# A quantized last layer on one NeuronCore: ScalarE writes the normalized rows, and the block maxima are taken over absolute values in one pass

## The reference

```python
def _mx_quantize(t, eps=1e-30):
    blocks = t.reshape(rows, K // 32, 32)
    scales = jnp.maximum(jnp.max(jnp.abs(blocks), axis=-1) / 7.5, eps)
    q = _nearest_on_grid(blocks / scales[..., None], _GRID)   # the 6-bit grid E2M3
    return (q, scales)

x = x + L1_attn(layernorm(x))       # state-space layer: delta, decay, scan, output
x = x + L1_ffn(layernorm(x))        # xd = xq * xs, wd = wq * ws, xd @ wd.T + bias
```

## Time and profile before

| | us |
|---|---|
| three runs | 3044.51, 3052.33, 3056.43 (median 3052.33) |
| the profiled execution | 3045.67 |
| its span in the trace | 3043.5 |
| PE busy | 2498.7 (82%) |
| DVE busy | 2124.9 (70%) |
| ACT busy | 1605.3 (53%) |
| POOL busy | 1112.7 (37%) |

### The profile page before, as it was taken

The page is one execution under the profiler, slowest core; times in us unless marked ns, Lnnn a source line. Parts: engine busy times, 40 slices in busy tenths (PEclk is TensorE's granted clock), DMA queues, the critical chain, the costliest instruction groups (busy, mean ns, idle before and its releaser), DMA issues. The chain is left out here.

```text
span 3043.5 us, 109358 instructions
## 1 busy us (share of the span) xinstructions
PE 2498.7 (82%) x45968; PEld 1887.2 (62%) x45968; DVE 2124.9 (70%) x5160; ACT 1605.3 (53%) x2896; POOL 1112.7 (37%) x1092
## 2 busy tenths in 40 slices
PE   4578887788888878788778999999978898987665
PEld 2345555556565555555566888888867676765443
DVE  4878988899889999888835222222325676878996
ACT  5454555555465554455124555555546666665442
POOL 0000233333333333233433777777744333332000
PEclk8778888888888898788679999999999899999877
DMA  2000122122222122113235999998798575754431
GB/s 66 8 11 10 49 74 71 53 79 75 71 74 73 55 79 73 63 69 111 84 114 172 301 310 305 306 305 296 258 336 305 202 275 209 268 217 173 161 107 28
DMA packets 191579, 448.61 MB, mean 147 GB/s; under 512 B 34034, under 2 KB 83700, under 8 KB 182772
## 3 DMA queue, kind: packets, MB, share of 16 engines
q1 hardware_dynamic: 129652, 284.26, 28.5%
q0 software_dynamic: 52224, 148.97, 12.9%
q10 hardware_dynamic: 9216, 8.39, 0.9%
HBM read 266.07 MB, written 175.42 MB: 145 GB/s over the span
## 5 line engine op out<-in xcount | busy, mean ns | idle before, releaser
L1041 POOL DMA_INDIRECT scr_xs<-xn_r,idx x512 | 534.1, 1043 | 1136.8 <-PE ps L473 479.7
L1068 POOL DMA_INDIRECT scr_ys<-y,idx_t x576 | 578.4, 1004 | 548.0 <-ACT sg L1333 253.1
L712 PE MATMUL ps<-xT,wr 128*128 128x256 f32 (+1 forms) x2560 | 563.5, 364 | 4.7 <-DVE h L2053 4.7
L2053 DVE TENSOR_TENSOR h<-sg,ps 128x256 f32<-128x256 f32 x320 | 125.2, 393 | 532.8 <-ACT sg L1333 532.2
L712 PEld LDWEIGHTS ps<-xT,wr 128*128 128x128 f32 x2560 | 439.1, 193 | 56.1 <-issue 14.1
L720 PE MATMUL ps<-wr,h 128*128 128x256 f32 x1152 | 312.3, 390 | 56.4 <-ACT y L1340 56.3
L1340 ACT ACTIVATE y<-ps,of_row 128x256 f32<-128x256 f32 x576 | 244.8, 471 | 145.2 <-PE ps L720 139.8
L720 PEld LDWEIGHTS ps<-wr,h 128*128 128x128 f32 x1152 | 218.5, 195 | 89.3 <-issue 62.1
L1680 DVE TENSOR_TENSOR tu<-tu,tmp 128x60 f32<-128x60 f32 (+14 forms) x480 | 242.5, 505 | 16.5
L527 PE MATMUL ps<-sq,w_proj 128*128 128x512 f32 x512 | 249.7, 624 | 5.1 <-issue 2.4
L1677 DVE TENSOR_TENSOR tmp<-tu 128x60 f32<-128x60 f32 (+14 forms) x480 | 241.6, 503 | 13.4
(11 more groups left out here) (268 smaller groups left out, 4231.6 us busy)
## 6 DMA issues: line engine op xcount, KB each, us to landing
wr<-in_wexp SPq DMA_DIRECT2D x224, 384.0 KB, 4.5
xt<-scr_xs SPq DMA_DIRECT2D x256, 280.0 KB, 4.2
yg<-scr_ys SPq DMA_DIRECT2D x64, 1024.0 KB, 7.4
scr_ys<-y,idx_t POOLq DMA_INDIRECT x576
scr_xs<-zeros SPq DMA_DIRECT2D x64, 140.0 KB
xt<-scr_xs SPq DMA_DIRECT2D x64, 140.0 KB
x_in<-in_x SPq DMA_DIRECT2D x64, 128.0 KB, 3.1
x_res<-in_x SPq DMA_DIRECT2D x64, 128.0 KB, 2.6
```

The costliest lines, as they stand in the source:

```text
L712: last = pe.matmul(ps[:, bank, half * TILE:half * TILE + wide], wr[:, w % NW, at:at + EI], xT2[:, t % NH, k, 0:wide], start=k == 0, stop=k ...
L1041: nc.gpsimd.indirect_dma_start(xs[int(i >= FIRST)][:, :], bass.IndirectOffsetOnAxis(idx[:, i % NR, c, k:k + 1], 0), xn_r[:, i % NR, c, :], ...
L1068: nc.gpsimd.indirect_dma_start(ys[int(t >= NTH[0])][:, :], bass.IndirectOffsetOnAxis(idx_t[:, t % NRT, r:r + 1], 0), y2[:, t % NY, r, :], ...
```

## The change

The four normalizing instructions of a round go from VectorE to ScalarE, which computes `x * std + off` with `off = -mean * std` in place of `(x - mean) * std`. VectorE therefore makes `off` for the quantized layer with a new small instruction (`quant_offsets`), between the tail statistics and `add("QO", i - 1)`. ScalarE's new `quant_rows(i)` stands behind the two roots and ahead of `share(2)` and `tail_rows(i + 1)`, and waits for `off` and for the turns of the `xq` before. VectorE waits for the rows on a new semaphore ahead of `quantize`. In `quantize`, the masking of the sign bit into `qb` and the maximum over `qb` become one reduction over `qa` with `apply_absolute_value`; this holds for the weight too.

```diff
+            def quant_rows(i):
+                if i:
+                    ring.filled(act, "QT1", i - 1)
+                act.wait_ge(s_off["quant"], i + 1)
+                for c in range(NC):
+                    last = nc.scalar.activation(xq[:, c, :], x3[:, i % NX3, c, :], ACT.Identity,
+                                                bias=off["quant"][:, c:c + 1], scale=std["quant"][:, c:c + 1])
+                last.then_inc(s_rows, 1)
...
                 root("quant", i)
                 if i + 1 < NB:
                     root("tail", i + 1)
+                quant_rows(i)
                 share(2)
                 if i + 1 < NB:
                     tail_rows(i + 1)
...
-            def normalize(dst, src, ph, i, st):
-                dve.wait_ge(s_std[ph], i + 1)
-                for c in range(NC):
-                    last = V.tensor_scalar(dst[:, c, :], src[:, c, :], mv[ph][:, c, 0:1],
-                                           std[ph][:, c:c + 1], ALU.subtract, ALU.mult)
-                    if c < NC - 1:
-                        st.did(last)
-                return last
...
-                st.did(V.tensor_scalar(qb.bitcast(I32), qa.bitcast(I32), 0x7FFFFFFF, None, ALU.bitwise_and))
-                st.wait(dve)
-                st.did(V.tensor_reduce(qs[:, 0:n, 0], blk(qb), AX.X, ALU.max))
+                st.did(V.tensor_reduce(qs[:, 0:n, 0], blk(qa), AX.X, ALU.max, apply_absolute_value=True))
                 st.wait(dve)
...
+            def quant_offsets(i):
+                offsets("quant", i)
+
             def quant_rows(i):
-                if i:
-                    ring.filled(dve, "QT1", i - 1)
-                sQ.did(normalize(xq, x3[:, i % NX3], "quant", i, sQ))
                 share(1)
-                sQ.wait(dve)
+                dve.wait_ge(s_rows, i + 1)
                 quantize(xq[:].rearrange("p c d -> p (c d)"), qb[:], qc[:], NC * D // QB, sQ, share)\
                     .then_inc(s_xn["quant"], 1)
...
                 share(1)
+                quant_offsets(i)
                 if i:
                     add("QO", i - 1)
```

More of the change, by code:

```diff
@@ L370, in network_kernel @@
         s_route = sem("s_route")
+        s_rows = sem("s_rows")
         s_x1 = sem("s_x1")
```

## The result

The kernel after takes 3059.68 us in the median of 20 runs against 3051.17 us for 20 runs of the kernel before beside it: ratio 1.0031, 95% interval 1.0021 to 1.0042, so 9.5 us more by the ratio (6 to 13; the medians are 8.5 apart). I had forecast 3077 us, +24.6, with a range of 3055 to 3097. The median lies inside the range, near its lower end, and the sign is right; the size is two and a half times too large. The ratio's interval lies above 1, so the loss is real, though smaller than the 15 us that I had said a measurement could tell from no change. The profiled execution took 3059.06 us, 13.4 more than that of before.

The account below looks back on a forecast made before the run. The bound was taken as a ring of waits through ScalarE, VectorE and TensorE; 10.4 + 2.4 + 6.8 + 7.1 - 2.1 = +24.6 us on the 3052.33 us median gave 3077 us, range 3055 to 3097.

Parts of the forecast that it names:

- the ring: Tail rounds: chain of engines waiting on each other, statistics to `xa` included; four added ScalarE activations, 2.07 to 2.08 us, delay it.
- Round 0 and the odd rounds: Rounds 0, 1, 3, 5, 7: ScalarE has no gap before `xa`, so 2.09 us each passes on in full, 10.4 us.
- The even rounds: Rounds 2, 4, 6, 8: ScalarE had 1.69 us to spare ahead of `xa`, so only 0.6 us each, 2.4 us.
- The clock in the mixed stage: Rounds 1 to 8: longer waits for `xa` lower TensorE's clock, 1.7 us in four of the eight, 6.8 us.
- The bare stage: Rounds 9 to 14, running alone: `xa` 1.47 us later each, 8.8 us less 1.8 of scan slack, +7.1 us; clock 0.
- VectorE's saving: About 2.0 us less VectorE work a round, 32 us over 16 rounds, worth 0 except in round 15.
- The end: Round 15: the removed normalizing and mask are on the path, 1.41 + 0.73 us, so -2.1 us.
- The one-pass maximum: In `quantize`: absolute-value reduction taken as 1.22 us, bounds 0.69 and 1.91; only round 15 would feel it, -0.5 to +0.7 us.
- (b): Rival for the whole tail: the order costs but TensorE's clock doesn't, +17.8 us, 3070 us; chance 0.22.
- The no-change form of (a): Rival: VectorE's saving gains in rounds 9 to 15 alone, cancelling the +12.8 us of earlier rounds, 3051 us; chance 0.10.
- VectorE as the bound everywhere: Rival: VectorE sets the time in all rounds, so its 32 us less work is gained, 3020 us; chance 0.05.
- The short form: Rival's part for rounds 9 to 15: VectorE's saving counts there, 6 x -2.0 - 2.1 = -14 us; no-change chance 0.10.

Follow-up runs that it names:

- `mixed_only`: Changed kernel with ScalarE writing the normalized rows in rounds 0 to 8 alone, VectorE normalizing in 9 to 15, sign mask kept: ratio 1.0034 to before.
- `late_mixed`: Rows on ScalarE in rounds 0 to 8 alone, mask kept, but placed behind the copies of the turned `xa`, ahead of softplus: ratio 0.9998 to before.
- `double`: Changed kernel with ScalarE writing the four rows once more each round into a tile that nobody reads: ratio 1.0163 to before.
- `before_again`: The kernel before, unchanged, traced a second time: 208.6 us from scan 9 to scan 15, against 208.5 in the first trace.
- `half_bare`: Rounds 0 to 8 as before; in 9 to 15 ScalarE writes the four rows plus two again into an unread tile: ratio 1.004 to before.
- `bare_only`: Changed kernel with ScalarE writing the rows in rounds 9 to 15 alone, rounds 0 to 8 and the mask as before: ratio 0.9993 to before.
- `abs_only`: The kernel before with only the one-pass reduction over absolute values in place of mask and maximum: ratio 1.0002 to before.
- `behind`: Changed kernel with ScalarE's rows directly behind the next block's `xa`, ahead of the copies of its turns, in all rounds: ratio 1.0057 to before.
- `best_dve`: Before with one-pass maximum; rounds 10 to 15 reordered (tail root and `xa` first, one table load dropped, `combine`s moved), VectorE normalizing throughout: 3031.98 us, ratio 0.9967.

## Why the prediction was right in sign and wrong in size

**ScalarE's rows sit on the ring: right.** The four activations took 2.06 us (forecast 2.07 to 2.08), need no table load, and `xa` follows them. `mixed_only` and `late_mixed` show that the place ahead of `sg`, `y` and `xa` is the whole cost of the mixed stage. VectorE's wait after softplus grew to 8.18 us in round 1, not to the 9.5 that I gave: part of what it lost went to the earlier waits for `sg` (2.05 and 3.08 us), worth nothing as forecast.

**Round 0 and the odd rounds: nearly right, and luck in the figure.** 10.4 us forecast; 0.9, 1.9, 1.9, 2.0 and 3.7 are 10.4 us, but some 1.7 us of it is the clock of round 7, which is another term of the sum. Without it 8.7 us are left, most of the difference in round 0, which became 0.9 us longer instead of 2.09.

**The even rounds: too high.** 2.4 us forecast, 0.3 measured (+0.5, -0.3, +0.4, -0.3). There the two waits together remain as long as the one was (1.97 to 2.01, 1.97 to 2.04, 1.97 to 2.23, 2.19 to 2.05 us); what `sg` loses is taken from the wait for `xa`.

**The clock in the mixed stage: the step that failed.** "Waits for `xa` up to 2 us mostly kept the higher level; now they will be 2.2 to 3.1 us." They were 0 to 1.7 us. The whole delay was there, 2.68 us in round 1, but in two pieces with matmuls between, since I had listed `y` among what stands behind the rows on ScalarE and then asked only who waits for `sg` and for `xa`. TensorE waits for `y` as well, and earlier. Of the four new falls at 1.7 us each one came, 1.7 of 6.8 us; round 4's low spell moved from the wait for `xa` to that for `y` and stayed one. No run has an undivided wait of this length in this very place. The nearest are the waits of 2.83 to 3.29 us for `y` in `double`, after three of which out of four the clock was low, so the division is the likely reason and isn't shown apart. How far a low spell is chance, before itself shows: its round 4 lost the clock after 1.97 us in one trace (transposes 1.92 us) and kept it after the same 1.97 us in `before_again` (1.09). The Trainium skill, "TensorE: Matmul & The Clock Gate", section "HAM oscillation — how this bites in real kernels", tells of idle gaps in a loop that make TensorE fall to half rate; here the pair of 1.88 and 0.80 us did not, that of 2.44 and 1.02 did, and the rounds of `half_bare` show that the time lost at a fall isn't the same each time.

**The bare stage: the rows right, their effect wrong.** 7.1 us forecast, 3.3 measured, and rounds of 35.5 us forecast where 34.1 came. The 1.47 us of each round are 1.24: the rows begin 0.1 us before the root's recorded end (2992.50 and 2992.59), and `xa` begins 1.96 us behind them, not 2.08. What failed is "In the bare stage the clock is low after each such wait already, 0 to 3 us more; I take 0." Less than nothing wasn't in the bounds. Over the six rounds the two products are 2.0 us shorter than in before, 1.2 us in each of the last two. The rest of the difference, 5.3 us, is six times 1.24 less 2.1 of slack, close to my 1.8 (8.8 - 1.8 is 7.0, where I had written 7.1). VectorE's saving was off the path in after, whose scans 10 to 14 wait 1.1 to 1.7 us for `d_a`. Nor is the 3.3 us a property of ScalarE's rows that I can separate: `bare_only` has 3.9 us with the rows alone, `abs_only` 3.4 in its one trace without them, through a lower clock, and neither shows in a ratio.

**The end: the rows right, the gain covered by the clock.** The reduction of round 15 begins 0.60 us after the last residual (3024.64 and 3025.24) where it began 2.75 after it (3012.05 and 3014.80). That is the -2.1. But the last two products ran at the lower clock to the end, 2.07 and 3.78 us, where those of before ran at the full one (1.12 and 1.99); with the first pair 0.2 us longer that is +2.9, which makes +0.8 of it:

```profile
3024.64 0.69 DVE L2142 TENSOR_TENSOR x<-x,ps 128x512 f32<-128x512 f32 x1 [1.95 <-PE ps L819]
3025.24 1.21 DVE L1495 TENSOR_REDUCE qs<-xq 128x32 f32<-128x1024 f32 x1
...
3046.25 2.07 PE L810 MATMUL ps<-bias_row,ones_all 1*128 1x512 f32 x2
...
3048.25 3.78 PE L819 MATMUL ps<-w_quant,quantT 128*128 128x256 f32 x8
```

This isn't chance in one execution: `behind`, `double` and `half_bare`, which begin this reduction equally early, end in 42.2 to 42.6 us as well, where the kernels that leave the end as it was take 41.5 to 41.6. So the clock took back this term too, and I had given the end no clock term.

**The one-pass maximum: right.** 1.21 to 1.22 us for the reduction, the row that I took. The case that it works otherwise is out. The Trainium skill, "Vector Engine (DVE) Microarchitecture Reference", section 2.3, lists the absolute value as a mask that is written as a constant when the reduction is set up; that I read from it that there is no pass of its own agrees with these 1.22 us.

Of the rivals, (b), that the order costs and the clock doesn't, came nearest in its mechanism, at +17.8 us against a measured 9.5. The no-change form of (a), 3051 us, is as near in number, but not in mechanism. VectorE as the bound everywhere is out. The short form, a gain of 14 us in the bare stage and at the end, is refuted by `bare_only`: its share of that form was 8 us, its interval reaches 7 us of gain at most, and its bare stage was longer. `abs_only` shows no gain either. VectorE does decide before's rounds 10 to 12, at 33.6 us, until the ring takes over at 34.1.

## What to carry to other kernels

Work that moves to another engine costs what stands behind it in that engine's queue, not what it takes: the same four activations a round cost 10.7 us ahead of the tile's work and `xa`, and nothing that shows behind the copies. For each instruction that is made late, ask every engine for its first wait on it; a delay that meets an engine in two places is not one long wait. And where a ring of engines passes through one whose clock changes, neither a saving nor an added microsecond can be carried through as itself: compare the settled rounds with the pieces that the clock stretches taken off. Before a few microseconds in one trace are given a cause, look for other kernels with the same code in that stretch, as here in round 9.

## What the runs showed that I had not expected

With 0.7 us a round less on VectorE a stage was no shorter, and in the one trace longer: 211.9 instead of 208.6 us, with TensorE's granted clock in rounds 10 to 12 at 0.75 in place of 0.80 to 0.85. The same product of eight 128x512 matmuls, behind a wait for `xa` of 6.0 and of 7.1 us, took 5.30 and 6.74 us in two bare rounds of one kernel. In `best_dve`, where TensorE had no wait ahead of turning `xa` and one of 0.84 us ahead of the product, it took 3.67 us:

```profile
2937.31 3.67 PE L780 MATMUL ps<-xT,w_delta 128*128 128x512 f32 x8 [0.84 <-ACT xT L1141]
```

yet rounds 11 to 13 took 33.3 to 33.9 us and no scan waited for `d_a` in them: VectorE decided, and the higher clock bought nothing there.
